# A fused cross-attention and expert kernel: row evictions, low parts, the output part and stores moved within an attention slot

## The reference

```python
x = x + xattn(layernorm(x), ctx)      # layer norms of both inputs inside
x = x + ffn(layernorm(x))             # one shared expert, 8 routed experts, top 2

def xattn(latents, context):
    q = ln(latents) @ Wq;  k, v = split(ln(context) @ Wkv)
    k = rope(k, cos, sin)
    p = softmax(clip(q @ k.T / 8, -11, 11))
    return (p @ v) @ Wo + bo
```

## Time and profile before

| | |
|---|---|
| time, median of 3 runs | 2279.45 us (2276.21 to 2282.15) |
| the profiled execution's own time | 2279.45 us |
| its span, first to last instruction | 2277.8 us |
| TensorE matmul busy | 2176.3 us, 96% of the span |
| TensorE weight loads busy | 1590.5 us, 70% |
| VectorE busy | 1799.4 us, 79% |
| ScalarE busy | 1351.8 us, 59% |
| GpSimd busy | 290.9 us, 13% |
| mean granted TensorE clock | 0.98 of full speed |

### The profile page before, as it was taken

The page is one execution under the profiler, slowest core; times in us unless marked ns, Lnnn a source line. Parts: engine busy times, 40 slices in busy tenths (PEclk is TensorE's granted clock), DMA queues, the critical chain, the costliest instruction groups (busy, mean ns, idle before and its releaser), DMA issues. The chain is left out here.

```text
span 2277.8 us, 48796 instructions
## 1 busy us (share of the span) xinstructions
PE 2176.3 (96%) x18002; PEld 1590.5 (70%) x18002; DVE 1799.4 (79%) x2416; ACT 1351.8 (59%) x1914; POOL 290.9 (13%) x300
## 2 busy tenths in 40 slices
PE   6999999999999999999999999999649999999998
PEld 5666666666666666666666666648538899999997
DVE  7999999889899899998988988994214555557777
ACT  5675675666567567566656655553114556557773
POOL 2010010000001011000001100003740111112210
PEclk9999999999999999999999999999769999999999
DMA  7245235235334423523533541233532433436656
GB/s 259 87 129 151 87 110 182 82 100 171 100 95 137 144 84 118 172 82 109 174 94 92 165 128 56 70 126 130 175 141 75 137 132 125 134 121 224 216 193 264
DMA packets 149314, 305.62 MB, mean 134 GB/s; under 512 B 34784, under 2 KB 71776, under 8 KB 146080
## 3 DMA queue, kind: packets, MB, share of 16 engines
q1 hardware_dynamic: 138688, 272.46, 38.0%
q0 software_dynamic: 10176, 30.45, 3.7%
q10 hardware_dynamic: 288, 0.26, 0.0%
HBM read 189.31 MB, written 79.20 MB: 118 GB/s over the span
## 5 line engine op out<-in xcount | busy, mean ns | idle before, releaser
L1030 ACT ACTIVATE probs<-scores 128x1024 f32<-128x1024 f32 x512 | 503.7, 1025 | 330.6 <-PE scores L745 325.3
L871 PE MATMUL sum_ps<-probs,v_nat 128*64 128x512 f32 x2056 | 479.9, 600 | 10.3 <-DVE probs L1229 10.3
L1335 DVE TENSOR_TENSOR sums<-sums,probs 128x1024 f32<-128x1024 f32 x384 | 470.1, 1224 | 12.5
L745 PE MATMUL scores<-q_split,k_split 64*128 64x512 f32 x3072 | 416.4, 395 | 1.8 <-ACT probs L1030 1.8
L1917 PE MATMUL sum_ps<-down,hid_split 128*128 128x256 f32 x2640 | 363.7, 286 | 48.2 <-issue 39.6
L1917 PEld LDWEIGHTS sum_ps<-down,hid_split 128*128 128x128 f32 x2640 | 347.0, 193 | 70.9 <-issue 52.1
L1229 DVE TENSOR_SCALAR probs<-probs 128x2048 f32<-128x2048 f32 x256 | 312.9, 1222 | 101.6 <-ACT probs L1030 99.9
L1894 PE MATMUL scores<-xT,up 128*128 128x512 f32 (+1 forms) x1680 | 353.9, 352 | 10.5 <-issue 10.4
L2051 DVE TENSOR_TENSOR hid_split<-hid,hid_split 128x512 fp32r<-128x512 f32 x205 | 141.9, 692 | 269.6 <-ACT hid_split L1981 246.3
L1980 ACT ACTIVATE hid<-scores 128x512 f32<-128x512 f32 x220 | 131.5, 598 | 325.6 <-PE scores L1894 241.9
L745 PEld LDWEIGHTS scores<-q_split,k_split 64*128 64x128 f32 x3072 | 283.5, 186 | 57.2 <-ACT probs L1030 5.9
(11 more groups left out here) (228 smaller groups left out, 2186.6 us busy)
## 6 DMA issues: line engine op xcount, KB each, us to landing
k_two<-k_two SPq DMA_DIRECT2D x252, 128.0 KB, 2.3
w_all<-wpack SPq DMA_DIRECT2D x60, 512.0 KB, 4.2
raw<-L_ffn_routed_up SPq DMA_DIRECT2D x27, 1024.0 KB
raw<-L_ffn_routed_down SPq DMA_DIRECT2D x27, 1024.0 KB
rden<-rden_rows SPq DMA_DIRECT2D x128, 128.0 KB, 2.9
ctx_parts<-stage SPq DMA_DIRECT2D x28, 512.0 KB, 3.4
ctx_all<-ctx_parts SPq DMA_DIRECT2D x14, 1024.0 KB, 7.0
sorted_rows<-zero POOLq DMA_DIRECT2D x64, 162.5 KB, 2.5
```

Of the source, the lines that this page charges most:

```text
L745: last = pe.matmul(scores[j % 2][:, head], k_split[i][own, a, j * P:(j + 1) * P], q_split[i][own, m], start=n == 0, stop=n == 2)
L871: last = pe.matmul(sum_ps[64 * head:64 * head + 64, p % 2], v_nat[p // 2 % 2][:, j, cols:cols + 64], probs[:, j % PROBS, head], start=j == ...
L1030: act.activation(probs[:, j % PROBS], scores[j % 2][:], ACT.Exp, scale=float(HD) ** -0.5).then_inc(s_exp, 1)
L1335: v.tensor_tensor(to, to, probs[:, j % PROBS], ALU.add).then_inc(s_add, 1)
```

## The change

Four edits, all in the `slot` functions of attention.

1. ScalarE: both halves of the rows are evicted in one go, directly after the keys. `high_of_next` comes behind them. The exponential of tile 2 comes ahead of `copy_values`, that of tile 3 behind it. In the last batch's slot 7, `split_weights(act, 2)` comes ahead of both.
2. VectorE: `low_stages` moves from ahead of `times_cos` to behind `add_rope`.
3. VectorE: `out_part` and its waits move ahead of `clip(6)` (and ahead of `split_weights` in the last batch).
4. SP: the stores of the staged rows move from behind `spread_den` to the end of the slot, behind the load of weights.

```diff
@@ sync, slot @@
                 store_norm((b + (B - 1)) % B, b + 1, result_norm(b))
-            for place in (1, 2):
-                stores(place)
             if p == 2 and not last(b):
...
                 first_rows()
+            stores(1)
+            stores(2)
@@ scalar, slot @@
-            def evict(kinds, only=None):
+            def evict(kinds):
                 for i, (place, kind, n) in enumerate(plan(b, p)):
-                    if kind not in kinds or only not in (None, place):
+                    if kind not in kinds:
                         continue
...
             exps(0, 1)
             evict("k")
+            evict("cxt")
             if not (last(b) and p == PAIRS - 1):
                 high_of_next()
-            evict("cxt", 1)
+            if last(b) and p == PAIRS - 1:
+                split_weights(act, 2)
+            exps(2)
 
             act.wait_ge(s_pv, b * (PAIRS * STEPS) + (G + PROBS))
             act.wait_ge(s_o, b * PAIRS + (p + 1))
             copy_values(before_p)
-            evict("cxt", 2)
-            if last(b) and p == PAIRS - 1:
-                split_weights(act, 2)
-            exps(2, 3)
+            exps(3)
             act.wait_ge(s_den, b * PAIRS + (p + 1))
@@ vector, slot @@
             add_up(3)
-            low_stages()
             if has(b, p, "k"):
...
                 add_rope()
+            low_stages()
             if p == NORMS:
...
-            if last(b) and p == PAIRS - 2:
-                split_weights(v, 1)
-            if last(b) and p == PAIRS - 1:
-                split_weights(v, 3)
-                split_weights(v, 4)
-
-            clip(6)
             if p == 1:
...
                 out_part(Y_SLOT[p], 0)
+            if last(b) and p == PAIRS - 2:
+                split_weights(v, 1)
+            if last(b) and p == PAIRS - 1:
+                split_weights(v, 3)
+                split_weights(v, 4)
+
+            clip(6)
             add_up(6)
```

## The result

| | before | after |
|---|---|---|
| median of 4 runs each | 2280.80 us (2276.21 to 2284.06) | 2312.39 us (2308.96 to 2318.35) |
| profiled execution | 2279.45 us, clock 0.980 | 2294.93 us, clock 0.985 |
| span of it | 2277.8 us | 2293.3 us |
| last value products of attention (L871) start | 1535.75 us | 1561.46 us |

The change makes the kernel slower: ratio 1.0143 [1.0114, 1.0171], 31.6 us between the medians, where the forecast said 2314.5 us. The four timed runs had spans of 2307.3 to 2316.7 us at a mean clock of 0.975 to 0.978. The profiled execution, at 0.985, is 14 to 23 us shorter than they are, so a trace and a median have to be joined with care.

A forecast was written before the change was run, and what follows sets the result against it. TensorE was taken as the bound in attention, under way for 185.69 of 187.40 us per batch. The forecast was 2279.45 + 23 (waits at full clock) + 12 (lost clock) = 2314.5 us, range 2297 to 2330 us.

The forecast's parts named there:

- Slot 1, +0.45: In slot 1, L936 waits for the later `copy_values` and starts at 638.12 against 637.67: 0.45 us later.
- Slot 2, +0.54: In slot 2, L936 waits for the later `copy_values` and starts at 662.94 against 662.40: 0.54 us later.
- Slots 6 and 7, +0.1 each: L936 delayed by the later copy: 0.09 us in slot 6, with its shorter row activations, and 0.1 in slot 7.
- the rows can't start earlier than today: On ScalarE, row activations wait for the transposes, which in slot 1 end at 634.16, with the first activation at 634.29.
- Slot 3, +1.79: In slot 3, with two halves of rows ahead of the copy, L936 starts at 689.30 against 687.51: 1.79 us later.
- Slots 3 to 5, 2.1 together: Net loss per batch: TensorE's 3.44 us delay less 1.18 of clip waits, 2.26; VectorE 2.0 to 2.1 late; 2.1 taken.
- Edit 4, counted 0 with 1 us per batch as the upper end: Slot 3's later stores land at 707.2 to 708.2, some tenths early or late for slot 4's rows: 0, at most 1 us.
- Edits 2 and 3, nothing: Later low parts on VectorE worth nothing; `out_part` ahead of `clip(6)` counted 0, between -0.5 and +0.5 us per batch.
- The clock, 12 us with 0 and 24 as the ends: Half of 14 new TensorE idle times in slots 3 and 4 lose the full clock, 1.7 us each: 12 us.
- the waits, 23: At the full clock, 1.2 + 2.1 = 3.3 us per batch in 7 batches of attention: 23 us.
- all 14 lose the clock: Every new idle time in slots 3 and 4 loses clock, 24 us, plus up to 7 for stores: 2326 to 2333; chance 0.15.
- Rival 3: Slot 3's copy still done by 687.5, `clip(4)` 1.2 us ahead, waits of slots 4 and 5 go: 2271 us; chance 0.04.

The follow-up runs named there:

- the second profile of the changed kernel: The whole change, all four edits, run once more for another profile, against the kernel before: 2259.27 us, ratio 1.0144.
- the version meant for use: Kernel before with both row halves ahead of the copy in slots 3 and 4, and slot 4's low parts made and stored in slot 5: 2293.97 us, 1.0072.
- the second group: Second of three groups of follow-up runs, each with its own runs of the unchanged kernel; here their median is 2227.49 us (21 runs).
- the third: Third of three groups of follow-up runs, each with its own runs of the unchanged kernel; here their median is 2278.74 us (20 runs).

## Why the prediction came out right, step by step

The mechanism was the predicted one and the median lies 2.1 us below the forecast. The forecast was a difference of 35 us, the measured one between the medians is 31.6. The terms of the sum did not all come out.

- **Slot 1, +0.45:** +0.44, idle time 0.40 (predicted 0.4). **Slot 2, +0.54:** +0.35, idle time 0.30. **Slots 6 and 7, +0.1 each:** +0.09 and 0. These made 1.2 us per batch and measure 0.9. The chain was right, and one premise was not: that the rows can't start earlier than today because they wait for the transposes. In slots 2 and 7 they waited for the high part of the keys. With it behind them they start (batch 3) 6.17 us into slot 2, where they started at 6.37, and 6.19 into slot 7 in place of 6.41. That is the 0.2 by which slot 2 is better than the forecast. The signal to TensorE, 0.05 in the sum, shows as 0.06.
- **Slot 3, +1.79:** +1.78, idle time 1.73 in every batch. `clip(4)` stands 0.63, predicted 0.65.
- **Slots 3 to 5, 2.1 together:** 2.0 where edit 1 stands alone (1.78 + 1.16 - 0.94), so the working from two sides holds. With all four edits it is 2.78 (1.78 + 1.89 - 0.89).
- **Edit 4, counted 0 with 1 us per batch as the upper end,** is a term that was mis-sized, by 0.8 us per batch. The stores go out 25.6 us into slot 3, and I had 26. But I let them land in 4.2 us, and after the change the view of the DMAs says:

```profile
lat_parts<-stage SPq DMA_DIRECT2D x14, 512.0 KB, 5.5
```

  With these, the first buffer was 0.8 us late for slot 4. Why they take longer stays open. At the end of the slot the stores stand directly behind the load of weights and the spreading of the reciprocals, but the place in the queue is not shown to be the cause: at the old place the median is 3.8 us with edit 1 alone, but 5.2 us where the exponential of tile 2 alone was moved, and 5.3 us where it was moved together with the high part of the keys. At the old place this doesn't matter, because the stores go out 17 to 18 us into slot 3, some 8 us earlier. So edit 1 alone has no such wait, and edits 2 to 4 without edit 1 have it and no loss. This part of the cost takes edit 1 and edit 4 together.
- **Edits 2 and 3, nothing:** shown for 3 (1.0119 against 1.0112). Edit 2 is a small gain beside edit 4, and no loss shows in the run with 2, 3 and 4.
- **The clock, 12 us with 0 and 24 as the ends.** Two windows of the profile after, 5 us each from the start of an idle time, with the granted clock as the third number from the end:

```profile
124.89:129.89 5.00, 3.27 (x35) 2.85 (x36) 3.49 (x3) 2.90 (x5) 1.11 (x2) 0.76 0.11 37
149.82:154.82 5.00, 2.51 (x37) 2.05 (x38) 4.03 (x12) 3.67 (x6) 3.44 (x3) 1.00 0.01 4
```

  An idle time of 1.73 lost the clock (a mean of 0.66 in the 5 us behind it, so 1.2 GHz for most of them), and one of 2.49 in the next slot did not. In this profile one of 14 lost it, which is 1.5 us (that slot 3 is 24.97 long in place of 23.44). By the mean clocks the timed runs lost 51 - 46 = 5 us more than before, good to some 2 us, and no row says how much of it lies in attention. So 12 was too much by some 7 us, and the waits, 23, too little by 3 to 4 (25.6 by the medians of the slots, 27.4 at the full clock): the two errors cancel in part. That the total is only 2 us off is partly luck. The assumption that the length of the idle time decides, with a bound between 1.39 and 1.89 us, was wrong: in the second profile of the changed kernel the same wait of 1.89 us for `x_all` is followed by the full clock.
- The rule of the Trainium skill in "TensorE: Matmul & The Clock Gate", section "A second HAM failure mode: psum-queue depth-cycling", read so that all 14 lose the clock, is not borne out: it was 1 and 5 of 14 in the two profiles of this kernel.
- **Rival 3,** that the copy is in time and VectorE gets ahead, needed a shorter row of work than edit 1 makes. With the exponential of tile 2 alone ahead of the copy its direction holds: the copy is in time, the exponentials come earlier and the waits for clips shrink, and the kernel is 4.7 us faster, where the rival had 8. The rival's 1.2 us from `clip(4)` is not part of that run.

## What to carry to other kernels

When work is moved ahead of an instruction that another engine waits for, add up the whole row of work from the last event that cannot move (here the end of the transposes) to that instruction, and compare it with when the waiting engine gets there. Each move may fit the slack by itself and the sum not: try them apart. For a store that is moved, follow both ends: what stands before it in its queue at the new place, who wants the buffer back, and who reads from memory what it writes. Don't take its time to landing as fixed: it was 3.8 to 5.5 us for the same store in these kernels.

## What the runs showed of the hardware that was not expected

- **Whether an idle time costs the clock is not decided by its length alone in this range.** Counted over five profiles (the change twice, edit 1, edits 1 and 3, edits 1 and 4), idle times of 1.72 to 1.74 us were followed by a reduced clock in 9 of 49 cases, those of 2.2 to 3.3 us in 8 of 21. With the copy ahead of both exponentials it was 4 of 4 for 2.0 to 2.6 us, in the version meant for use 3 of 7 for 2.8 to 3.3 us, and behind the 2.3 us of the very first slot 5 of all 14 profiles. The longer ones lost it more often. Each case cost about 1.5 us in slot 3 (24.97 against 23.44). What decides stays open; the same program at the same place differs from one execution to the next: in the 5 us from the start of the wait of slot 4 in the first batch the clock was 1.00 in one profile of the changed kernel and 0.73 in the other:

```profile
148.44:153.44 5.00, 2.53 (x23) 1.72 (x24) 4.05 (x12) 3.71 (x6) 3.45 (x3) 0.73 0.02 3
```

- **GpSimd slows VectorE far more than its busy time says:** two subtractions of 128x512 (1.3 to 2.3 us each) made two additions of 128x1024 take up to 4.43 us rather than 2.48. A single addition beside one takes 2.20 us, where it takes 1.23 alone.
- **The groups of runs differ by 50 us in the same kernel** (2229 and 2279 us), and not in attention. In a profile of the second group the last value products of attention start at 1531.87 us and the last matmul at 2212.59; in one of the third they start at 1533.44 and 2263.64. The 50 us lie in the expert part. From 1600 to 1700 us TensorE is busy 85.17 us at a mean clock of 0.93 in the former and 48.39 us at 0.66 in the latter. The record names another chip for each group. What makes the difference was not tried.
